# A four-layer WKV and feed-forward stack on one core: the third denominator's inversion moved behind the first two SiLU tiles, and fillers put into a gap of TensorE

## What is computed

```
# condition of layer l, channels c, tokens t, per batch
ek = exp(min(k,30));  ekv = ek*k;  euk = exp(min(u+k,30))
num = forward_scan(ekv) + backward_scan(ekv) - ekv + euk*k
den = forward_scan(ek)  + backward_scan(ek)  - ek  + euk
y   = sigmoid(x) * num / max(den, 1e-8) * (0.8 + 0.2*tf)
# feed-forward net of layer 0: three ternary weight matrices, 8-bit tokens
q  = round(rmsnorm(y) * 127/absmax);  w = round(w/mean|w|) clipped to -1, 0, 1
z  = silu(q @ w_gate) * (q @ w_up)         # 1024 hidden
x += round(rmsnorm(z) * 127/absmax) @ w_down
# layer 1: 8 experts, the best two of each token; layer 2: 8-bit gated net; layer 3: block-quantised GELU net
```

## Time and profile before

| | before |
|---|---|
| three executions | 417.19, 419.41, 421.05 us (median 419.41) |
| profiled execution | 420.55 us, of which 418.8 us is the span of the trace |
| TensorE busy | 365.4 us (87%) |
| VectorE busy | 335.6 us (80%) |
| ScalarE busy | 288.2 us (69%) |
| GpSimd busy | 90.6 us (22%) |
| chain of work that ended last | PE 63%, DVE 15%, ACT 12%, issue 5% |
| mean granted TensorE clock | 0.959 of full |

### The profile page before, as it was taken

How to read it: one execution, slowest core, us unless ns; L and a number is a source line. 1 busy time by engine, 2 the same in 40 slices (tenths; PEclk the granted TensorE clock), 3 DMA queues, 4 the chain that set the end, 5 groups by cost and what they waited for, 6 DMA issues and landing times.

```text
span 418.8 us, 7035 instructions
## 1 busy us (share of the span) xinstructions
PE 365.4 (87%) x2477; PEld 311.2 (74%) x2489; DVE 335.6 (80%) x493; ACT 288.2 (69%) x512; POOL 90.6 (22%) x105
## 2 busy tenths in 40 slices
PE   3994558779786779999999999999998998999885
PEld 0994435548664479999999999999987787887543
DVE  4999866999876999999999940499603688899986
ACT  5999857996965368676676767576643455688873
POOL 4000300000030234352523322356641000000000
PEclk9898588989996999999999999999999999999999
DMA  7700000000058266711171179483002400000002
GB/s 270 260 0 2 1 0 0 2 0 2 1 181 297 58 234 212 253 40 39 38 239 41 38 239 329 154 257 116 25 15 76 152 0 2 1 2 0 2 26 77
DMA packets 22690, 38.54 MB, mean 92 GB/s; under 512 B 2088, under 2 KB 17080, under 8 KB 22528
## 3 DMA queue, kind: packets, MB, share of 16 engines
q1 hardware_dynamic: 17120, 24.98, 17.7%
q0 software_dynamic: 2528, 7.08, 5.1%
q10 hardware_dynamic: 3008, 6.03, 4.1%
HBM read 32.97 MB, written 5.11 MB: 91 GB/s over the span
## 4 chain that ended last, share of the span: by engine, by line
PE 63%; DVE 15%; ACT 12%; issue 5%; DMA 2%; ACTq 1%; SPq 0%; DVEq 0%
PE bank L1795 20%; PE bank L1773 19%; PE bank L1591 8%; PE bank L1858 3%; PE bank L1625 2%; PE bank L1848 2%; DVE big L1286 1%; ACT yT L549 1%; PE bank L1765 1%; DVE scr L879 1%; DMA v<-in_kT 1%; DMA g<-choice_rows 1%; PE bank L1643 1%; ACT big L561 1%; ACT big L739 1%
## 5 line engine op out<-in xcount | busy, mean ns | idle before, releaser
L1773 PE MATMUL bank<-big,yT 128*128 x368 | 83.3, 379 | 0.0
L634 ACT ACTIVATE yT<-bank,big 128x128 f32<-128x128 f32 x184 | 52.5, 369 | 42.9 <-PE bank L1795 42.9
L1773 PEld LDWEIGHTS bank<-big,yT 128*128 128x128 f32 x368 | 68.1, 190 | 8.8 <-issue 0.4
L383 POOL TENSOR_TENSOR small<-small 128x2 f32<-128x2 f32 (+1 forms) x9 | 9.6, 1072 | 168.6 <-DVE small L1321 70.8
L431 POOL DMA_INDIRECT choice_rows<-yo,rowo x23 | 30.6, 1329 | 62.4 <-ACT yo L643 53.4
L416 POOL DMA_INDIRECT xg<-token_rows,rowi x23 | 32.3, 1402 | 54.3 <-PE bank L1765 34.6
L1795 PEld LDWEIGHTS bank<-ygT,big 128*128 128x128 f32 x256 | 29.8, 192 | 1.9 <-issue 1.6
L1795 PE MATMUL bank<-ygT,big 128*128 128x128 f32 x256 | 29.9, 275 | 1.4 <-ACT ygT L626 1.4
L1795 PEld LDWEIGHTS bank<-ygT,w3T 128*128 128x128 f32 x256 | 29.7, 192 | 1.6 <-issue 1.3
L1795 PE MATMUL bank<-ygT,w3T 128*128 128x128 f32 x256 | 29.9, 275 | 0.9 <-ACT ygT L626 0.9
L1603 PE MATMUL bank<-zeros,identb 128*128 128x512 bf16 x84 | 23.7, 423 | 7.6 <-POOL identb L379 5.4
(11 more groups left out here) (371 smaller groups left out, 821.3 us busy)
## 6 DMA issues: line engine op xcount, KB each, us to landing
big<-in_moe_w SPq DMA_DIRECT2D x16, 1024.0 KB, 6.9
v<-in_kT SPq DMA_DIRECT2D x2, 512.0 KB, 4.5
big<-in_gateT SPq DMA_DIRECT2D x1, 1024.0 KB, 7.0
big<-in_upT SPq DMA_DIRECT2D x1, 1024.0 KB, 9.1
big<-in_downT SPq DMA_DIRECT2D x1, 1024.0 KB, 11.3
x<-in_x_bsc SPq DMA_DIRECT2D x1, 1024.0 KB, 13.7
token_rows<-y POOLq DMA_DIRECT2D x4, 256.0 KB, 7.9
ek<-in_w3a ACTq DMA_DIRECT2D x1, 1024.0 KB, 7.2
```

What stands on the lines that cost most here:

```text
L634: ins = sc.activation(hT[j % 2][:, c], ps[1 + 2 * (j % 2) + c // 4][:, (c % 4) * P:(c % 4 + 1) * P], ACT.Gelu, bias=b1s[:, c, j:j + 1])
L1773: ins = te.matmul(ps[5 + 2 * (j % 2)][:, 0:C], hT[j % 2][:, c], big[:, bass.ds(at + (W2_AT + c * C), C)], start=(c == 0), stop=(c == IC - 1))
```

## The change

Five places are edited:

- On ScalarE `euk(3)` and `invert(2)` leave their place before the SiLUs of pair 0 and go behind those of tiles 0 and 1. The ln/exp set has to be loaded for them and the SiLU set again behind them.
- `ternary(2)` is split. Its first instruction goes ahead of the first SiLU, its second behind the SiLUs of pair 1.
- On DVE `newton(2)` goes from between `gate_z(0)` and `gate_z(1)` to behind the scale of pair 0, ahead of `newton_end(2)`.
- On TensorE part 2 of the third denominator goes behind `gate_up(0, 1)`; 24 fillers are put behind part 0; the wait for `num_used` goes up to the fillers, and `turn(0)` in pair 1 waits for `newton(2)`.
- In pair 3 the ln/exp table load goes behind `evict(5)`.

```diff
-            euk(3)
-            invert(2)
             sc.preload_act_table(ACT.Silu)
+            ternary_magic(2).then_inc(s["wd_magic"], 1)
             act.wait_ge(s["fx_ready"], 1)
...
                 silu(b)
                 if p == 0:
-                    ternary(2)
+                    sc.preload_act_table_set("natural_log_exp_and_others")
+                    euk(3)
+                    invert(2)
+                    sc.preload_act_table(ACT.Silu)
+                elif p == 1:
+                    act.wait_ge(s["wd_magic"], 1)
+                    ternary_sign(2)
...
                 square(b)
+                if p >= 1:
+                    evict(b - 2)
                 if p == T // 2 - 1:
                     sc.preload_act_table_set("natural_log_exp_and_others")
-                if p >= 1:
-                    evict(b - 2)
...
                 gate_z(a)
-                if p == 0:
-                    newton(2)
-                else:
+                if p >= 1:
                     down_scale(p - 1)
...
                 if p == 0:
+                    newton(2)
                     newton_end(2)
...
             add_up(0, 2, 0, True, tuple(range(T)))
+            pe.wait_ge(s["num_used"], 1)
+            keep_clock(2, 24)
...
-            add_up(0, 2, 2, True, tuple(range(T)))
             pe.wait_ge(s["w_ternary"], 2)
             gate_up(0, 0)
             gate_up(0, 1)
+            add_up(0, 2, 2, True, tuple(range(T)))
             gate_up(1, 0)
             gate_up(1, 1)
-            pe.wait_ge(s["num_used"], 1)
...
                 gate_up(b, 1)
+                if p == 1:
+                    pe.wait_ge(s["dc_ready"], 3)
                 turn(a - 2)
```

More of the change, by code:

```diff
@@ L220, in bass_adaln_ffn_stack @@
             down_ready q2T_last x_l0 sig1 yT_ready rh_ready rh_gelu logits lg_shift lg_exp last_gelu last_sum last_ps last_row  masks_ready             gate_ready gcT_tr gcT_ready ps1_ready ps2_ready bias_ready l1_done             w3q w3t w3_copy l2_int xt2_tr sig2 y2_ready y2h_ready y2T_ready gu2_ready silu2_ready h2_ready down2 x_l2             r3_tr r3_copy sig3 y3_ready var3 pow3 hq3 hq3_tr hq3T u3_ready a3_ready g3_ready q3_ready
-            q3_tr q3T_ready d3_ready ob_ready x_done stored w3_copy2 r3_copy2 bias_added br_ready b1_ready ld_b1 b1_turned b1s_ready w1_ready y1_stored a_ready b_ready rows_ps rows_ready ek_free zero_row""".split()
+            q3_tr q3T_ready d3_ready ob_ready x_done stored w3_copy2 r3_copy2 bias_added br_ready b1_ready ld_b1 b1_turned b1s_ready w1_ready y1_stored a_ready b_ready rows_ps rows_ready ek_free zero_row wd_magic""".split()
         s = {n: sem(n) for n in NAMES}
@@ L479, in invert_last, with ternary_magic, ternary_sign @@
                 sc.activation(r0[3], r0[3], ACT.Exp, scale=-1.0).then_inc(s["r0_ready"], 1)
-            def ternary(m):
+            def ternary_magic(m):
+                src = wgu[:, m] if m < 2 else wd
+                return sc.activation(src, src, ACT.Identity, bias=magic[:, 0:1], scale=wscale[:, m:m + 1])
+            def ternary_sign(m):
                 src = wgu[:, m] if m < 2 else wd
                 dst = wgu_t[:, m] if m < 2 else wd_t
-                link(sc.activation(src, src, ACT.Identity, bias=magic[:, 0:1], scale=wscale[:, m:m + 1]))
                 sc.activation(dst, src, ACT.Sign, bias=magic[:, 1:2]).then_inc(s["w_ternary"], 1)
@@ L519, in _ @@
             act.wait_ge(s["wscale_ready"], 1)
-            ternary(0)
+            link(ternary_magic(0))
+            ternary_sign(0)
             decay_of(2)
-            ternary(1)
+            link(ternary_magic(1))
+            ternary_sign(1)
             act.wait_ge(s["y0_ready"], KC)
```

## The result

Over 13 executions of each the changed kernel takes 422.25 us in the median (421.27 to 426.9) and the kernel before 420.48 (417.19 to 426.31). The ratio is 1.0074, 95% interval 1.0047 to 1.0101: slower by 0.7%, 3.1 us by the ratio. Timed again beside other kernels it gave 1.0062 (1.0035 to 1.0088). The forecast was 421.8 us and 0.6%. The ratio leaves out the one slow execution of the kernel before (426.31) and keeps the changed kernel's 426.9; without that one too the plain means differ by 2.7 us, and the medians differ by 1.8.

The account below looks back on a forecast made before the run. A chain of waits through the layer 0 net, changing engines, was taken as the bound, not any engine's busy share; -4.46 + 3.19 + 1.69 + 1.91 = +2.33 us gave 421.8 us, range 418.2 to 424.5.

Parts of the forecast that it names:

- The products of the first two tiles: Layer 0 net, tiles 0 and 1: first product at 58.77, fourth SiLU half at 61.52 instead of 65.98, 4.46 us earlier.
- What stands behind them: ScalarE behind the fourth SiLU half: two table loads, euk(3) and inversion replace the ternary pair, 3.19 us more.
- The clock after the third gap: TensorE ahead of tile 3's gate_up: gap grows from 2.73 to 6.3 us, clock 0.50 at 73.20, costing 1.69 us.
- The second ternary instruction: ScalarE, between tile 3's SiLU and offset(1): not hidden, its slot of 1.91 us delays tile 4.
- The fillers at 0: 24 fillers in TensorE's first gap end near 41.8, 5.0 us before the transposes: gain 0, cost 0.
- The sum: At tile 4's SiLU: -4.46 + 3.19 + 1.69 + 1.91 = +2.33 us; kernel forecast 421.8 us, 0.6% slower.
- reach the end one for one: Layer 0 net onward: what the net loses or gains by 120 us moves everything behind it equally.
- the rival in which the delay is soaked up: Later in the net, a half-clock stretch may be missed: up to 2.3 us back, 419.5 us; chance 0.08.
- The clock held in the 1.92 us gap: Rival for TensorE's short gap, 57.6 to 59.6: clock falls there too, 1.69 us more, 423.5 us; chance 0.2.
- The fillers did not hold it to the transposes: Rival at 46.80: fillers hold the clock at 1.00 to the transposes, all 1.9 us earlier, 419.9 us; chance 0.12.

Follow-up runs that it names:

- both sets of fillers: Kernel before with 44 fillers in the first gap and 7 instead of 4 ahead of layer 2, nothing reordered: ratio 0.9999, median 419.69 us.
- all three edits: Changed kernel with second ternary instruction early, 44 fillers in first gap, second gap filled: ratio 0.9940, 417.86 us; with 7 fillers ahead of layer 2: 0.9934.

## Why the prediction was right

- **The products of the first two tiles.** Forecast: 4.46 us earlier at the fourth SiLU half, held by VectorE's sweep. Measured: 19.18 us behind the first transpose before (65.98 and 46.80), 14.68 after (61.86 and 47.18), 4.50 earlier, the product directly behind the sweep.
- **What stands behind them.** Forecast 3.19. From the fourth SiLU half to tile 2's SiLU it was 6.89 us (65.98 to 72.87) and is 10.18 (61.86 to 72.04): 3.29.
- **The clock after the third gap.** Forecast a gap of 6.3 us, 0.50, and 1.69. Measured 6.52 us, 0.50, and 1.69 (5.21 against 3.52 between tile 2's SiLU and the second half of tile 3). Filling the gap takes 1.68 off.
- **The second ternary instruction.** Forecast 1.91. Measured 9.01 - 7.12 = 1.89, and 1.75 come back when it is moved.
- **The fillers at 0.** Shown: the clock is at 0.50 from 46.8 on, the idle gap behind them 5.11 us, and without them nothing measurable changes.
- **The sum.** Forecast +2.33 at tile 4, measured 39.08 - 36.71 = +2.37. The time of 421.8 stood on the median of three executions, 419.41; thirteen have 420.48. So the difference is the better test: 2.4 us forecast.
- **What went in by luck.** I took the delay to reach the end one for one. In the two first traces it doesn't: at the net's end only 0.7 of the 2.4 us are left. The kernel before has a stretch at half clock from 90.8 to 94.2 there, and the changed one runs at full, though TensorE had stood still for the same 2.18 us in both. The kernel before and then the changed one, of each TensorE's timeline row behind the gap and the stretch from 90.8 to 94.2:

```profile
90.08 1.23 PE L1625 MATMUL bank<-big 128*128 128x512 bf16 x4 [2.18 <-DVE big L1020]
90.80:94.20 3.40, 3.18 (x13) 2.32 (x13) 3.33 (x5) 3.13 (x6) 0.00 (x0) 0.50 0.00 0
```

```profile
92.83 1.02 PE L1636 MATMUL bank<-big 128*128 128x512 bf16 x4 [2.18 <-DVE big L1030]
90.80:94.20 3.40, 1.37 (x9) 0.97 (x10) 3.40 (x4) 3.40 (x6) 0.00 (x0) 1.00 0.00 0
```

  This is the rival in which the delay is soaked up, and in this pair of traces it happened. In the second trace of the changed kernel two such stretches came back, and its net is 1.9 us longer than before's. The times say that on the whole the delay isn't soaked up: 1.8 us by the medians, 2.7 by the plain means without the longest execution of each, 3.1 by the ratio (2.0 to 4.2). The forecast 2.33 lies among them, and they don't size it more closely.
- **The rivals.** The clock held in the 1.92 us gap, in all eleven traces of the changed order. The fillers did not hold it to the transposes.

Still open is why the net's 3.1 us of the kernel before with both sets of fillers show in no time, while a net of the same length in the kernel with all three edits gives 0.66%. The two traces differ in the stage ahead of the first transposes (47.97 and 46.72, same code) and from the bias matmuls to the first `gate_up_l2` (8.1 and 7.5 us), but one trace of each doesn't show that this is so in every execution. Nor does the kernel before have one time. Of its 17 executions beside these, three took 417.8 to 418.1 us with a mean clock of 0.975, and twelve 420.4 to 421.5 with 0.953 to 0.967; the profiled one (420.55, 0.959) is like the twelve, and no trace of the other kind was kept. So every distance here is measured against the longer kind.

## What to carry to other kernels

Work that is pulled forward on one engine lets the next one run ahead and then stand still longer: look for the gap that grows, and whether TensorE's clock survives it. Fillers have to reach up to the work that is to profit; ones that ended 5 us early were worth nothing here. And an instruction that comes off a cluster should go where its engine waits anyway: here ScalarE had waits of 1.88 and 3.87 us just ahead, and the changed kernel had put only the first half of the pair there, so that the second cost its full 1.9 us.

## What the runs showed of the hardware that I had not expected

- TensorE's clock stayed at 1.00 through 4.1 us of complete idleness (42.6 to 46.7) and was 0.50 when the work began at 46.8. At layer 2 it fell in or behind idle waits of 1.26 and 1.55 us among matmuls that use 16 of 128 rows, and held over one of 1.08 in the trace of all three edits. In pairs 2 and 3 it fell behind a gap of 2.18 us in the kernel before and held over the same 2.18 in the changed one. A gap's length alone doesn't say whether it falls.
- A gain in one stage was undone, in the execution profiled, by a clock fall in another 280 us later (10.1 us at 0.50, 3.3 us lost). A change of 2 us can't be judged from its own stage.
- With 44 fillers the fp32 transposes and sums ran at full clock from their first one on, and the unchanged order gained 3.0 us at tile 4, where I had estimated 1.9 for the changed one.
